# Where a four-node attention stage makes its rotary angles: remainders on GpSimd, Abs beside the sines, masks from two row groups

## What is computed

```
member = one_hot(top_k(x @ wr, 2)).sum() > 0            # per head: 2 of 4 nodes
pos = cumsum(member) - member                            # place of a token in each node
for n in range(4):
    c, s = cos_c[pos[..., n]], sin_c[pos[..., n]]
    qr = q * c + rotate_half(q) * s
    kr = k * c + rotate_half(k) * s
    scores = where(causal & member[..., n], qr @ kr.T * SCALE, NEG)
    outs.append(softmax(scores) @ v)
out = the two chosen nodes' outs, weighted by softmax(top_k values)
```

## Time and profile before

| | us |
|---|---|
| median of 3 runs (1850.45 to 1855.61) | 1853.75 |
| profiled execution | 1856.05 |
| its span | 1854.3 |
| PE busy | 1372.8 |
| DVE busy | 1114.4 |
| ACT busy | 714.3 |
| POOL busy | 384.8 |

### The profile page before, as it was taken

One profiled execution on the slowest core, in us unless ns is written; L12 is line 12 of the kernel. 1 busy time (PEld: TensorE's weight loads), 2 busy tenths in 40 slices (PEclk: granted clock), 3 DMA queues, 4 the chain that ended last, 5 costly groups with the idle time before them and its releaser, 6 DMA issues. The chain is left out here.

```text
span 1854.3 us, 24940 instructions
## 1 busy us (share of the span) xinstructions
PE 1372.8 (74%) x8853; PEld 1037.9 (56%) x8853; DVE 1114.4 (60%) x2412; ACT 714.3 (39%) x1537; POOL 384.8 (21%) x400
## 2 busy tenths in 40 slices
PE   4898898888866897674674975758735977868785
PEld 3676666666745565561453964545623764744662
DVE  5899998999545576324556536443436648435634
ACT  4456666656313464232231221004102425645451
POOL 2565566665210100110101310000001000000000
PEclk8899899998878799796786986759967997989897
DMA  6011011010010100340002510000020002000100
GB/s 219 22 42 38 25 42 36 27 42 15 1 59 1 35 1 1 122 137 0 1 13 76 173 52 1 1 1 1 1 91 0 1 1 44 2 1 5 40 2 12
DMA packets 31611, 63.97 MB, mean 35 GB/s; under 512 B 6785, under 2 KB 18177, under 8 KB 30977
## 3 DMA queue, kind: packets, MB, share of 16 engines
q1 hardware_dynamic: 30464, 60.15, 10.5%
q0 software_dynamic: 1024, 2.23, 0.5%
HBM read 54.13 MB, written 4.18 MB: 31 GB/s over the span
## 5 line engine op out<-in xcount | busy, mean ns | idle before, releaser
L188 POOL TENSOR_TENSOR rstd<-spread,minus_half 128x4 f32<-128x4 f32 x36 | 36.8, 1023 | 1001.9 <-DVE spread L170 1001.9
L918 PE MATMUL l0h_scores<-l0h_k_rot,l0h_q_slots 128*128 128x128 f32 (+1 forms) x1024 | 206.6, 349 | 0.0
L918 PEld LDWEIGHTS l0h_scores<-l0h_k_rot,l0h_q_slots 128*128 128x128 f32 x1024 | 169.9, 208 | 13.1
L1135 POOL TENSOR_TENSOR l0h_k_part<-large_weights,l0h_sines 128x512 f32<-128x512 f32 x64 | 83.9, 1311 | 177.2 <-PE l0h_scores L918 129.1
L1009 ACT ACTIVATE l0h_scores<-l0h_scores,l0h_top 128x128 f32<-128x128 f32 (+1 forms) x256 | 100.4, 392 | 27.9 <-DVE l0h_top L1088 27.7
L1082 DVE TENSOR_TENSOR l0h_q_slots<-l0h_q_rot,l0h_chosen 128x1024 f32<-128x1024 f32 x64 | 78.4, 1225 | 6.7
L894 PE MATMUL l0h_projected<-XT,l0h_wq 128*128 128x256 f32 x256 | 70.2, 398 | 15.3 <-ACT large_weights L980 12.0
L908 PE MATMUL l0h_scores<-l0h_key_masks,l0h_query_picks 4*128 4x128 bf16 (+1 forms) x256 | 45.0, 257 | 49.2 <-DVE l0h_probs L1105 49.1
L1136 POOL TENSOR_TENSOR l0h_k_rot<-large_weights,l0h_cosines 128x512 f32<-128x512 f32 x64 | 80.9, 1264 | 0.0
L1088 DVE TENSOR_REDUCE l0h_top<-l0h_scores 128x2 f32<-128x256 f32 (+1 forms) x128 | 65.1, 548 | 6.4 <-PE l0h_scores L918 6.4
L1447 ACT ACTIVATE l0n_probs<-l0n_scores,l0n_top 128x256 f32<-128x256 f32 x128 | 53.8, 483 | 39.0 <-DVE l0n_top L1478 38.9
(11 more groups left out here) (762 smaller groups left out, 3585.8 us busy)
## 6 DMA issues: line engine op xcount, KB each, us to landing
l1e_experts<-in_l_experts SPq DMA_DIRECT2D x16, 768.0 KB, 4.3
l0e_experts<-in_l_experts SPq DMA_DIRECT2D x15, 578.0 KB, 4.0
l0h_chosen<-l0h_chosen_dram SPq DMA_DIRECT2D x64, 128.0 KB, 2.9
small_weights<-in_w_l_ffn SPq DMA_DIRECT2D x1, 4016.0 KB, 12.1
l0h_pos<-l0h_pos_dram SPq DMA_DIRECT2D x56, 64.0 KB, 2.0
large_weights<-in_w_l_xattn SPq DMA_DIRECT2D x1, 2632.0 KB, 9.0
l3f_late<-l3f_values SPq DMA_DIRECT2D x2, 1040.0 KB, 7.0
l0h_wq<-in_l_wq SPq DMA_DIRECT2D x16, 128.0 KB, 2.9
```

Of the source, the lines that this page charges most:

```text
L918: mm = nc.tensor.matmul(at[:, slot], q_slots[:, s % 2, slot, part, i * P:(i + 1) * P], k_rot[:, s % 2, part, 0:KEYS[i][1]], start=False, s ...
L1135: nc.gpsimd.tensor_tensor(k_part[:], source, at_batch(sines, s), ALU.mult)
```

## The change

It does three things. The two operations of `reduce_turns` go, for heads 2 to 15, from VectorE's step b = 3 to GpSimd's step b = 0, behind `rotate_k`, one head later in the loop (`reduce_turns(h + 1)` in head h where it was `reduce_turns(h + 2)`). ScalarE's `fold` goes from b = 3 to b = 0, right in front of `sines_of`. The masks are loaded twice, to partitions 0 to 3 and 64 to 67, by four DMAs per head instead of two; tile 0 reads the first and tile 1 the second copy, and the four mask matmuls of a step are issued alternately, ahead of everything else of the step.

```diff
-        key_masks = sb("key_masks", [NODES, 2, N], BF16)
-        query_picks = sb("query_picks", [NODES, 2, CHOICES, N], BF16)
+        key_masks = sb("key_masks", [P // 2 + NODES, 2, N], BF16)
+        query_picks = sb("query_picks", [P // 2 + NODES, 2, CHOICES, N], BF16)
+        rows_of_tile = lambda i: slice(i * P // 2, i * P // 2 + NODES)
@@ SP, load_masks
-                    sp.dma_start(key_masks[:, h % 2], absent_dram[h * NODES:(h + 1) * NODES])\
-                        .then_inc(masks_loaded[h % 2], 16)
-                    sp.dma_start(query_picks[:, h % 2],
-                                 chosen_dram[:, h * NODES:(h + 1) * NODES].rearrange("o r s -> r o s"))\
-                        .then_inc(masks_loaded[h % 2], 16)
+                    for i in range(TB):
+                        sp.dma_start(key_masks[rows_of_tile(i), h % 2], absent_dram[h * NODES:(h + 1) * NODES])\
+                            .then_inc(masks_loaded[h % 2], 16)
+                        sp.dma_start(query_picks[rows_of_tile(i), h % 2],
+                                     chosen_dram[:, h * NODES:(h + 1) * NODES].rearrange("o r s -> r o s"))\
+                            .then_inc(masks_loaded[h % 2], 16)
@@ TensorE, score
-                    pe.wait_ge(masks_loaded[h % 2], 32 * (h // 2 + 1))
+                    pe.wait_ge(masks_loaded[h % 2], 64 * (h // 2 + 1))
+                    for slot in range(CHOICES):
+                        for i in range(TB):
+                            query = slice((TB * b + i) * P, (TB * b + i + 1) * P)
+                            rows = rows_of_tile(i)
+                            nc.tensor.matmul(unit(scores, s, i)[:, slot], query_picks[rows, h % 2, slot, query],
+                                             key_masks[rows, h % 2, b * S:b * S + KEYS[i][1]], start=(slot == 0),
+                                             stop=False, skip_group_check=True)
                     for i in range(TB):
                         at = unit(scores, s, i)
-                        query = slice((TB * b + i) * P, (TB * b + i + 1) * P)
-                        for slot in range(CHOICES):
-                            nc.tensor.matmul(at[:, slot], query_picks[:, h % 2, slot, query],
-                                             key_masks[:, h % 2, b * S:b * S + KEYS[i][1]], start=(slot == 0), stop=False,
-                                             skip_group_check=True)
@@ ScalarE, step s
                     if b == 0 and 1 <= h < H0 - 1:
+                        fold(h + 1)
                         sines_of(h + 1)
                     if b == 2 and h + 2 < H0:
                         turns(h + 2)
-                    if b == 3 and h + 2 < H0:
-                        fold(h + 2)
@@ VectorE, step s
                     combine(s)
-                    if b == 3 and h + 2 < H0:
-                        reduce_turns(h + 2)
@@ GpSimd
+                def reduce_turns(h):
+                    g.wait_ge(turns_ready, h + 1)
+                    link(g, nc.gpsimd.tensor_scalar(sines[:, h % 2], cosines[:, h % 2], ROUND, ROUND, ALU.add, ALU.subtract))
+                    nc.gpsimd.tensor_tensor(sines[:, h % 2], sines[:, h % 2], cosines[:, h % 2], ALU.subtract)\
+                        .then_inc(turns_reduced, 1)
+
                 for s in range(STEPS):
+                    h, b = step(s)
                     rotate_k(s)
+                    if b == 0 and 1 <= h < H0 - 1:
+                        reduce_turns(h + 1)
```

## The result

The changed kernel takes **1948.33 us** in the median of five runs (1944.82 to 1951.01), against 1851.21 us for the kernel before on the same chip (five runs): a ratio of 1.0509, interval 1.0491 to 1.0528. That is 97 us slower, where 34 were forecast. The sign was right; the time lies 30 us above the top of the range.

The account below looks back on a forecast made before the run. VectorE sets the pace, 6.17 us a step. Six plain heads +16.6, head 1 +1.4, head 14 +5.6, head 0 -2.7 and key-copy pairs +13.4 sum to +34.3 us: 1888 us, range 1862 to 1918.

Parts of the forecast that it names:

- (1): VectorE: two remainder operations go from 14 heads, 33.9 us off, the gain if nothing else came late.
- (2): ScalarE, b = 0: Abs ahead of the sines becomes serial; VectorE newly waits 2.20 us in each head.
- (3): GpSimd, b = 0: remainder waits for turns and holds up b = 1's rotate_k; scores late by 2.6 us.
- R: Time the remainder's two operations take on GpSimd: 3.9 us, bounds 3.4 and 4.8.
- T2: Start of the maximum search of a head's third step; turns were to end 7.9 us behind it.
- T: Start of a head's first maximum search (b = 0); the next was put at T2 + 12.34 + 0.2.
- L: How much the first scores of b = 1 come too late: 2.6 us, bounds 2.1 to 3.5.
- Rival A: Stall in b = 0 also brings low clock to scores behind it: 1.6 us in 10 heads, 1904 us; chance 0.21.
- (4): TensorE masks from two row groups: 0.16 us off each b = 0, between 0 and 0.35.
- (5): TensorE idles before b = 3's scores, which run at 1.2 GHz: 1.0 us per head, bounds 0 and 1.3.
- rival B: GpSimd isn't late at the remainder, no lateness of scores: +2 us, 1856 us; chance 0.13.

Follow-up runs that it names:

- the last kernel: Changed kernel with turns at the end of b = 1, Abs and sines behind b = 0's exponentials (sines not in heads 3, 7, 11): 1813.93 us.
- both kernels that cure it: Changed kernel with remainders queued behind rotate_k of b = 1: 1847.25 us; or with turns issued in b = 1, not b = 2: 1846.27 us.
- the kernel with 384 columns: Changed kernel with GpSimd's tensor_scalar on 384 of 1024 columns, the other 640 getting a subtraction of an array from itself: 1901.81 us.

## Why the prediction was right, and where it was wrong

**What bounds the kernel: right.** VectorE sets the pace, 6.17 us a step; the version in which nothing else comes late goes exactly at it.

**(1), right.** The two operations are gone from b = 3, and with nothing else late a head takes 24.69 us in the last kernel, 2.4 less than the 27.10 that the prediction had added up (27.73 measured, with the low clock in it).

**(2), right.** The serial chain was put at 2.20 us per head; it is 1.89 in a plain head where it stands alone, and half of the 0.31 between is the masks (below).

**(3), the queue right, its price wrong.** That GpSimd would stand at the remainder, and rotate_k of b = 1 and TensorE behind it, is seen in all 14 heads, and both kernels that cure it, from either side, lose nothing. The failed term is tensor_scalar: 1.44 us taken, 2.35 (as for two inputs) as its upper bound, 3.63 measured. The value came from affine_select and memset on 128 columns, other instructions, and the bound from the belief that one input can't cost more than two. The trace of before held a warning: its one-input COPY on GpSimd (L1213, 128 x 16) takes 0.705 us, where a memset of 128 x 128 takes 0.204. So R was 6.1 instead of 3.9, and outside its bounds of 3.4 to 4.8. For head 6: turns end at T2 + 8.57 (forecast 7.9), the remainder takes 6.1 (3.9), T itself comes 0.6 later than forecast, and L is 255.16 - 249.58 - 0.64 = 4.94 instead of 2.6. In the heads behind a key copy, L grew alike: tile 0's scores of head 4 waited 2.5 us, where 0.4 was forecast.

The Trainium skill (GPSIMD Engine Reference, 3.1) has a body of k ≤ 2 at 1.03 cycles for an element and a two-input one at about 2.6; the estimates from them for 1024 elements are 0.9 and 2.2 us. The runs here don't agree with the first: 3.63 us for two operations and 2.78 for one are three to four times that. The second fits the 2.35 of tensor_tensor.

**Rival A was no rival but an addition.** This is the second step that failed: the forecast's sum put the clock behind the stall at nothing, held it for an alternative, and gave A 0.21 because the masks and the triangle run in between. They didn't help: the block of L922 takes 4.81 us in head 6 (255.16 to 259.97) instead of 2.9, 1.9 more, and in the kernel with 384 columns it was slow in ten of 14 heads. The earlier trace rows had shown the low clock behind 2.91 us of idle, and the forecast's own L of 2.6 was near it, so 0.21 was too low.

**(4), too small.** 0.16 us taken, 0.32 measured, inside 0 to 0.35. As the Trainium skill has it (TensorE: Matmul & The Clock Gate, Part 3), matmuls of different row groups run concurrently. The four in 0.39 us, where two of them alone took as long, agree.

**(5), right in size:** 1.0 taken; 0.67 is what is left for it in the sum below, and no run measured it by itself.

**The sum, with measured terms.** The reciprocal of b = 1 was put at T + 12.70. With L 4.94, the block's 1.9 and 0.16 more off for the masks it comes to 19.38, and the trace has 268.96 - 249.58 = 19.38. With the 1.84 from the reciprocal to the next maximum and two steps of 6.17 that makes 33.56, and head 6 took 283.81 - 249.58 = 34.23; the 0.67 between is put down to the clock in b = 3. So the sum of a plain head was built right and two of its terms were wrong. For the whole time it had a third, smaller error the other way: without lateness (rival B) it gave 2 us more than before, and the two kernels without lateness are 8 and 10 us below it. The masks, worth 10 us on their own, are the likely cause. In us: the kernel with the forecast's R is 46 above its before, 12 more than the 34.3 forecast, where rival A had been priced at 16; tensor_scalar's price is worth 48 more. That is 3.4 us for each of 14 heads, where R grew by 2.3; the rest was not taken apart.

**The range** reached from 1862 to 1918 and missed because the upper bound of R wasn't one. With 3.63 for tensor_scalar the same sum gives L about 4.8 and, with rival A, a plain head of 34.3 us, as measured (34.4). That the sign came out right was no luck: it hung on the queue, which both cures show.

## What to carry to other kernels

An operation whose input comes late belongs behind everything in its queue that others wait for: with the same two GpSimd operations the kernel lost 97 us when they stood ahead of one rotate_k and nothing when they stood behind it. Moving work off the pace-setting engine pays only when the chain that carries it is issued early too; here that made the difference between 1948 and 1814 us. A price that the trace doesn't show is bounded above by no neighbour of another kind, and a stall of TensorE is to be priced with the clock behind it.

## What the runs showed of the hardware that was not expected

- GpSimd's tensor_scalar on fp32 is dearer than tensor_tensor: 128 x 1024 in 3.63 us with two operations and 2.78 with one, against 2.35; 128 x 384 in 1.50 against 1.00.
- TensorE's granted clock was 0.50 (109.57 to 111.60 us of the kernel with 384 columns) behind an idle time of 2.48 us with five small bf16 matmuls just ahead of it. Matmuls whose result nobody reads, put into the stall, had the scores behind them run at 1.00 and made the kernel 26 us faster than after.
- Four mask matmuls of 4 rows, alternately from rows 0 and 64, take 0.39 us together, as long as the two of tile 1 alone, and with this order the step is 0.32 us shorter.
